# Graph stage of a graph/attention/expert layer: the edge part of the first layer computed for two node tiles at a time on 64-row halves, its bias added earlier

## The chip, the cores and the metric

The kernel runs on one core of one Trainium2 chip. The metric is the device time of one execution in microseconds (us). Three executions of the kernel before gave 1022.07, 1025.47 and 1028.08 us; the median, 1025.47 us, is the time before. All arithmetic named here is fp32 unless a row says bf16.

## The reference, cut to what matters

A layer over 3125 nodes with 256 features each, 53125 edges with 64 attributes each (`src` and `dst` node numbers), in four steps:

```python
xn = layernorm(x)                                   # 3125 x 256
# graph part
sums   = segment_sum(edge_attr, src, 3125)          # 3125 x 64
counts = segment_sum(ones, src, 3125)
agg    = sums / maximum(counts, 1)
h      = relu(concat([xn, agg, u[0] for every node])  W1 + b1)   # 448 -> 512
g      = h  W2 + b2                                # 512 -> 256
# linear-attention part over all nodes, 8 heads of 32
x      = x + g + attention(xn)
# expert part: router, softmax, best 2 of 8 experts, two-layer GELU network each
x      = x + moe(layernorm(x))
```

The rows of W1 fall into three blocks: 256 that multiply xn (the node part), 64 that multiply agg (the edge part) and 128 that multiply u[0] (the global part, the same for every node).

## The kernel before, in words

The 3125 nodes are 25 tiles of 125 (`T`, `P`). The whole program is written out by hand, one list of instructions for each engine, tied together by semaphores; there is no planner. The order is this.

- Edge sums, all the way to about 717 us. VectorE compares source numbers within groups of edges (`compare`, L1581), TensorE adds equal ones up (`dedup`, L1123), ScalarE copies the sums out (`sums_copy`, L750) and GpSimd scatter-adds each group of 128 edges to tables in HBM by an indirect DMA (L690, 368 of them).
- Beside it, first pass (25 tiles, to about 235 us): layernorm, keys and values, moments for the attention (VectorE's L1641 is its largest instruction). In tile 15 the global part is made: TensorE multiplies u0 by w1u, a row of 512 in PSUM (L1224), and VectorE adds it to the bias row, which lies as row 64 in `w1a` (L1698).
- Beside it, second pass (7 blocks of 3 or 4 tiles, in 56 rounds, to about 691 us): attention outputs. It also computes the node part of the graph layer: `hidden_x` (L1302) multiplies W1's node block with xn for a whole block of up to 500 nodes, a quarter (`m`) of the 512 outputs at a time, `h_copy` (L935) copies it from PSUM and a DMA stores it in HBM (`hpre_dram`, L938). The next `dedup` on TensorE waits for that copy, since it uses the same PSUM bank.
- When all scatters have landed, the tables are read back and averaged on VectorE (L1848 to L1859, `mean_ready`). TensorE turns the mean of each tile to 64 rows by 125 columns (L1434), ScalarE copies four tiles at a time to `aggT` (L1010), whose row 64 GpSimd set to one (L694).
- Graph stage (`gnn`, 25 tiles in a software pipeline of 29 iterations). In iteration t TensorE does `ha(t)` (L1445: 4 matmuls of 65 rows, w1a by aggT, 125 columns, into bank 1 or 2 in turn), `layer2(t-1)` (L1455, 4 matmuls of 128 rows, 256 columns), `tok_T(t-3)` (L1465) and `router(t-4)` (L1474). VectorE does `hsum(t)` (L1868: PSUM plus the stored node part, read back for two tiles at a time), `x2_of(t-1)` (L1875, then the statistics L1877 and L1879), `xl_of(t-2)` (L1887, L1888) and `lg_of(t-4)` (L1894). ScalarE does the ReLU (L1017), a square root (L1023) and two copies (L1030, L1037). `ha(t)` waits for `hsum(t-2)`, as each of its two banks holds one tile.
- Between iterations lies the routing of five batches of tiles (0-5, 6-11, 12-16, 17-21, 22-24): `lead`, `follow`, `weights` and `place` on VectorE in iterations t1+4 to t1+7 (L1911 to L1963), with t1 the end of the batch; an exponential on ScalarE (L1047), which needs another function table, and `ranks` on TensorE (L1489 to L1491).
- After `place` of a batch GpSimd sends its rows to the experts' regions, one indirect DMA for each tile and choice (L709, 50 in all). The expert stage (to the end) starts when the last has landed.

Of the kernel before, what the change touches and what calls it, by code (L numbers as in the profile page):

```python
# [9 lines left out]
ALU = mybir.AluOpType  # L10
# [4 lines left out]
def gps_layer(nc, x, src_col, src_row, edge_attr, u_in, W1, b1, W2, b2, WqkvT, bqkv, WprojT, bproj, temperature,  # L15
              routerT, ew1, eb1, ew2, eb2, out):
    N, C = x.shape
# [56 lines left out]
    with ctx:  # L74
        def sb(name, shape, dt=fp32):
            return ctx.enter_context(nc.sbuf_tensor(name, shape, dt))

        def sem(name):
            return ctx.enter_context(nc.semaphore(name))
# [23 lines left out]
        w1x = sb("w1x", [128, KC, HID])  # L103
        w1a = sb("w1a", [EA + 1, HID])
        w2s = sb("w2s", [128, MC, C])
# [114 lines left out]
        after_xl = r1_off[0]  # L220
        aggT = carve([EA + 1, T * P])
        cinv = carve([P, T])
# [94 lines left out]
        aggT_ready = sem("aggT_ready")  # L317
        agg_one = sem("agg_one")
        bias_ready = sem("bias_ready")
# [182 lines left out]
        def inside(t):  # L502
            return 0 <= t < T
# [6 lines left out]
        def _(sp):  # L510
# [45 lines left out]
            load_late(w1x[:, :, :], W1[0:C, :].rearrange("(k p) n -> p k n", p=128))  # L556
            load_late(w1a[0:EA, :], W1[C:C + EA, :])
            load_late(w1u[:, :], W1[C + EA:C + EA + 128, :])
            load_late(w1a[EA:EA + 1, :], b1.rearrange("(a n) -> a n", a=1))
            load_late(u0[:, :], u_in[0:1, :].rearrange("a p -> p a"), slow=True)  # L560
# [80 lines left out]
        def _(pool):  # L641
# [51 lines left out]
            pool.wait_ge(x1_ready, NP * NB)  # L693
            pool.memset(aggT[EA:EA + 1, :], 1.0).then_inc(agg_one, 1)  # L694
            for h in range(2):
# [31 lines left out]
        def _(act):  # L727
# [203 lines left out]
            def h_copy(b, m):  # L931
                n = width(b)
                act.wait_ge(h_ps, MC * b + m + 1)
                wait(act, hpre_stored[m % 2], 16 * (MC // 2 * b + m // 2))
                act.activation(hpre[:, m % 2, 0:n], bank(B0, 128, 0, n), ACT.Copy).then_inc(h_ready, 1)  # L935
                act.wait_ge(h_ready, MC * b + m + 1)
                c0 = BLK[b][0] * P
                act.dma_start(hpre_dram[:, m, c0:c0 + n], hpre[:, m % 2, 0:n]).then_inc(hpre_stored[m % 2], 16)  # L938
# [68 lines left out]
            for b in range(NBK):  # L1007
                nb = min(BPB, T - b * BPB) * P
                act.wait_ge(aggT_ps, b + 1)
                act.activation(aggT[0:EA, b * BPB * P:b * BPB * P + nb], bank((0, 7, 5, 6)[b % 4], EA, 0, nb),  # L1010
                               ACT.Copy).then_inc(aggT_ready, 1)
# [99 lines left out]
        def _(pe):  # L1111
# [104 lines left out]
            for t in range(T):  # L1216
# [5 lines left out]
                if t == 15:  # L1222
                    pe.wait_ge(w_loaded, 16 * 11)
                    mm(ps[EA:EA + 1, B1 * BANK:B1 * BANK + HID], lhsT=u0[:, :], rhs=w1u[:, :], start=True, stop=True).then_inc(brow_ps, 1)  # L1224
                if t == 16:
# [205 lines left out]
            for b in range(NBK):  # L1431
                wait(pe, aggT_ready, b - 3)
                for t in range(b * BPB, min((b + 1) * BPB, T)):
                    m = pe.transpose(bank((0, 7, 5, 6)[b % 4], EA, t % BPB * P, (t % BPB + 1) * P), table_sb(0)[:, t, 0:EA], ident[0:P, 0:P])  # L1434
                m.then_inc(aggT_ps, 1)
            pe.wait_ge(agg_one, 1)

            def ha(t, u):
                if not inside(t):
                    return  # L1440
                if t <= 1:
                    wait(pe, aggT_ready, NBK if t else 1)
                wait(pe, hsum_ready, t - 1)
                for m in range(MC):
                    z = mm(bank(1 + u, 128, m * P, (m + 1) * P), lhsT=w1a[:, m * 128:(m + 1) * 128], rhs=aggT[:, bass.ds(t * P, P)],  # L1445
                           start=True, stop=True)
                z.then_inc(ha_ps, 1)
# [29 lines left out]
            def gnn(t, u, k):  # L1477
                ha(t, u)
                layer2(t - 1, 1 - u)
                tok_T(t - 3, 1 - u)  # L1480
                router(t - 4, u)
# [74 lines left out]
        def _(v):  # L1556
# [126 lines left out]
            for t in range(T):  # L1683
# [10 lines left out]
                if t == 15:  # L1694
                    v.wait_ge(w_loaded, 16 * 11)
                    link(v.tensor_scalar(temp[:, :], temp[:, :], SC2, None, ALU.mult))
                    v.wait_ge(brow_ps, 1)
                    v.tensor_tensor(w1a[EA:EA + 1, :], ps[EA:EA + 1, B1 * BANK:B1 * BANK + HID], w1a[EA:EA + 1, :], ALU.add).then_inc(brow_read, 1)  # L1698
                if t in (17, 20):
# [162 lines left out]
            def hsum(t, u, k):  # L1862
                if not inside(t):
                    return
                wait(v, ha_ps, t + 1)
                wait(v, hpre_back[k % 2], k // 2 * 16 + 16)
                wait(v, gnn_ps, t - 1)
                v.tensor_tensor(hs[:, u, :].rearrange("p (m n) -> p m n", m=MC), bank(1 + u, 128, 0, MC * P).rearrange("p (m n) -> p m n", m=MC),  # L1868
                                hpre2[:, k % 2, :, u * P:(u + 1) * P], ALU.add).then_inc(hsum_ready, 1)

# [224 lines left out]
```

## Time and profile before

| | us |
|---|---|
| median of three executions | 1025.47 |
| the profiled execution: its time | 1024.87 |
| its span, first to last instruction | 1023.1 |
| busy in the span: TensorE (PE) / VectorE (DVE) / ScalarE (ACT) / GpSimd (POOL) | 844.8 / 627.1 / 416.3 / 710.3 |
| graph stage, by L1445's first and L1455's last start | 740.7 to 830.4 |
| mean granted TensorE clock | 0.904 |

Times in the rows below are microseconds from the start of the span unless marked ns. The granted clock is a share of full speed and has two levels, 1.00 (2.4 GHz) and 0.50 (1.2 GHz); a number between them is a mean over a stretch. The profile records an fp32 matmul as two instructions, each streaming its columns once; this text calls each a pass. PEld is TensorE's loading of weights. The time outside the span, 1.8 us, is start and end of the program.

### The profile page before, as it was taken

What the parts mean: (1) busy time and instruction counts of PE and PEld (TensorE: products, weight loads), DVE (VectorE), ACT (ScalarE), POOL (GpSimd) and SP (SyncE); (2) the same over time, 40 slices, a digit from 0 to 9 for tenths busy, and PEclk for the clock granted to TensorE, in tenths of its full rate; (3) what the DMA queues carried; (4) which work ended last, traced back from release to release, by engine and by line L of the source; (5) the groups of instructions that cost most, each with busy time, mean ns of one, the idle gap of its engine ahead of it and who ended that gap; (6) DMA issues with size and microseconds to landing.
All of it is one profiled execution on the core that took longest, in us unless ns stands there. A gap on an engine that the chain in (4) does not pass through costs nothing.

```text
span 1023.1 us, 19212 instructions
## 1 busy us (share of the span) xinstructions
PE 844.8 (83%) x6172; PEld 520.5 (51%) x6172; DVE 627.1 (61%) x2123; ACT 416.3 (41%) x1087; POOL 710.3 (69%) x511
## 2 busy tenths in 40 slices
PE   3888888979999999999999999990299961999930
PEld 2434333435445545544455555550288851899930
DVE  3899997994665464454645646650567773655534
ACT  3554553332554334343343434330145440666620
POOL 4688888888888888887788888888312568544430
PEclk7799998996999999999999999995599975999975
DMA  9865663555655554555555555334952424344449
GB/s 288 196 108 81 94 117 41 81 88 76 129 74 81 111 92 67 69 86 100 100 88 80 106 83 110 42 28 42 274 170 82 145 88 135 107 132 125 130 131 276
DMA packets 146342, 113.86 MB, mean 111 GB/s; under 512 B 109023, under 2 KB 132131, under 8 KB 146118
## 3 DMA queue, kind: packets, MB, share of 16 engines
q1 hardware_dynamic: 81156, 72.53, 25.3%
q0 software_dynamic: 58080, 25.70, 24.2%
q10 hardware_dynamic: 7010, 14.42, 4.4%
q8 instruction: 52, 0.85, 0.4%
q14 instruction: 44, 0.36, 0.1%
HBM read 72.52 MB, written 41.17 MB: 111 GB/s over the span
## 4 chain that ended last, share of the span: by engine, by line
PE 42%; DVE 20%; POOL 19%; issue 9%; DMA 6%; ACT 3%; ACTq 0%; SPq 0%; POOLq 0%; DVEq 0%
POOL edge_sums L690 17%; DVE r2t L1641 9%; PE ps L1315 5%; PE ps L1526 5%; PE ps L1537 5%; PE ps L1123 4%; DVE same L1581 3%; PE ps L1455 3%; PE ps L1251 3%; PE ps L1302 3%; DMA r2t<-expert_outputs 2%; PE ps L1265 2%; POOL routed_rows L709 2%; PE ps L1191 1%; DMA edges<-in_edge_attr 1%
## 5 line engine op out<-in xcount | busy, mean ns | idle before, releaser
L690 POOL DMA_INDIRECT edge_sums<-sums,addr x368 | 576.3, 1566 | 135.2 <-issue 108.8
L1678 DVE TENSOR_SCALAR oh<-node,dsrc 128x500 bf16<-128x500 int16 (+1 forms) x336 | 100.6, 360 | 49.8 <-PE ps L1315 49.1
L916 ACT ACTIVATE r<-ps 128x500 f32<-128x500 f32 (+1 forms) x224 | 103.4, 548 | 66.8 <-PE ps L1251 66.7
L1315 PE MATMUL ps<-oh,r2t 128*64 128x500 bf16 (+1 forms) x1008 | 114.6, 360 | 1.5 <-DVE oh L1678 1.4
L1123 PE MATMUL ps<-edges,same 128*128 128x65 f32 x736 | 103.5, 287 | 10.4 <-ACT sums L750 6.2
L1123 PEld LDWEIGHTS ps<-edges,same 128*128 128x128 f32 x736 | 93.9, 200 | 34.8 <-issue 19.1
L1641 DVE TENSOR_TENSOR r2t<-ps,r 125x4096 f32<-125x4096 f32 x25 | 110.3, 4413 | 0.0
L1581 DVE SCALAR_TENSOR_TENSOR same<-srow,src_f,below 128x128 f32<-128x128 int32 x368 | 105.7, 344 | 6.7 <-DMA srow<-in_src_row 5.3
L721 POOL DMA_INDIRECT expert_outputs<-r x56 | 54.5, 974 | 55.9 <-DVE r L2034 49.5
L1170 PE MATMUL ps<-r2t,r 125*32 125x512 f32 x400 | 60.7, 732 | 31.4 <-DVE r2t L1641 31.4
L1315 PEld LDWEIGHTS ps<-oh,r2t 128*64 128x64 bf16 x1008 | 49.6, 110 | 64.8 <-issue 38.7
L750 ACT ACTIVATE sums<-ps 128x260 f32<-128x260 f32 x92 | 36.5, 398 | 109.0 <-PE ps L1123 105.6
L709 POOL DMA_INDIRECT routed_rows<-r,row_idx x25 | 24.7, 988 | 59.3 <-ACT edges L1037 41.0
L1526 PE MATMUL ps<-r 128*128 128x128 f32 x448 | 60.8, 279 | 1.5 <-ACT r L1072 1.5
L1251 PE MATMUL ps<-r,pick 32*128 32x500 f32 (+1 forms) x448 | 61.1, 591 | 0.0
L1537 PE MATMUL ps<-r2t,r 128*128 x224 | 57.6, 380 | 0.0
L1526 PEld LDWEIGHTS ps<-r 128*128 128x128 f32 x448 | 56.1, 196 | 2.0 <-ACT r L1063 1.1
L1265 PE MATMUL ps<-r,mq 128*32 128x500 f32 (+1 forms) x448 | 53.6, 550 | 0.0
L2024 DVE COPY r<-r2t 128x512 f32 x56 | 33.4, 596 | 32.7 <-issue 17.7
L1161 PE MATMUL ps<-wqkv,r 128*125 128x512 f32 x100 | 53.2, 656 | 0.0
L1455 PE MATMUL ps<-w2s,r 128*125 128x256 f32 x200 | 48.9, 388 | 4.0 <-ACT r L1017 4.0
L1072 ACT ACTIVATE r<-ps,step_bias 128x128 f32<-128x128 f32 x112 | 35.2, 366 | 38.6 <-PE ps L1537 38.6
(284 smaller groups left out, 1377.2 us busy)
## 6 DMA issues: line engine op xcount, KB each, us to landing
srow<-in_src_row SPq DMA_DIRECT2D x46, 512.0 KB, 6.1
edges<-in_edge_attr SPq DMA_DIRECT2D x23, 512.0 KB
r<-routed_rows SPq DMA_DIRECT2D x56, 129.0 KB, 2.1
r<-hpre_rows SPq DMA_DIRECT2D x12, 500.0 KB, 4.2
edge_sums<-sums,addr POOLq DMA_INDIRECT x368, 3.2
r2t<-in_ew SPq DMA_DIRECT2D x4, 1024.0 KB, 10.0
hpre_rows<-r ACTq DMA_DIRECT2D x16, 250.0 KB, 2.3
edge_sums<-r SPq DMA_DIRECT2D x4, 884.0 KB, 14.3
```

What stands on the lines that cost most here:

```text
L690: pool.indirect_dma_start(out=tables[k], out_offset=bass.IndirectOffsetOnAxis(ap=addr[:, j:j + 1], axis=0), in_=sums[:, j % OR, :], in_off ...
L916: act.activation(phT[:, R % 2, h, 0:n], bank(BP[h], 128, 0, n), ACT.Square).then_inc(pair_squares, 1)
L1123: m = mm(bank(b, 128, k * F, (k + 1) * F), lhsT=same[:, j % SR, :], rhs=edges[:, h, j % CH, :], start=True, stop=True)
L1251: m = mm(bank(BP[h], 128, 0, n), lhsT=pick2[D * h:D * (h + 1), c * 128:(c + 1) * 128], rhs=qnT[D * h:D * (h + 1), b % 2, g, 0:n], start=Tr ...
L1265: m = mm(ps[D * h:D * (h + 1), BY * BANK:BY * BANK + n], lhsT=mq[:, g, c, D * h:D * (h + 1)], rhs=phT[:, R % 2, h, 0:n], start=False, stop ...
L1315: m = mm(ps[EA * a:EA * (a + 1), BD * BANK:BD * BANK + n], lhsT=parts3[:, (DCH - 1 - 2 * w // DW) * DW + (2 * w + a) % DW, s, :], rhs=oh[: ...
L1455: z = mm(bank(3 + u, P, 0, C), lhsT=hs[:, u, m * P:(m + 1) * P], rhs=w2s[:, m, :], start=(m == 0), stop=(m == MC - 1))
L1526: z = mm(bank(2 + h % 2, 128, m * 128, (m + 1) * 128), lhsT=w1_now[:, h % 2, k, m * 128:(m + 1) * 128], rhs=xsT[:, h % 2, k * 128:(k + 1) ...
L1537: z = mm(bank(6 + h % 2, 128, 0, C), lhsT=hT[:, h % 2, k * 128:(k + 1) * 128], rhs=ew2_s[:, k, bass.ds(col, C)], start=(k == 0), stop=(k = ...
L1581: v.scalar_tensor_tensor(same[:, j % SR, :], srow[:, c % 2, j % RH * 128:(j % RH + 1) * 128], src_f[:, j:j + 1], below[:, :], ALU.is_equal ...
L1641: v.tensor_tensor(phi[:, u], heads(bank(BK[u], P, 0, C), None).unsqueeze(2).to_broadcast([P, H, OFF, D]), turned(kdup[:, u, :, :], 1, H, 2 ...
L1678: v.tensor_scalar(oh[:, (2 * i + a) % OHS, 0:nt * P].rearrange("p (t n) -> p t n", t=nt), node16[:, 0:nt, :], dsrc[:, 2 * w + a:2 * w + a ...
```

## The change

1. `aggT` holds each tile's mean twice, on rows 0 to 63 and 64 to 127, and so does `w1a` with W1's edge block (a second load). The row of ones is gone. To get the two copies in PSUM, the transpose L1434 becomes two ordinary products with the identity, one on array columns 0 to 63, one on 64 to 127. ScalarE's L1010 copies 128 rows instead of 64.
2. `ha(k)` computes a pair of tiles in every other iteration: again 4 matmuls, now of 64 rows and 250 columns, quarters 0 and 2 on the array's rows 0 to 63 into bank 1, quarters 1 and 3 on rows 64 to 127 into bank 2. It waits until `hsum` has read both tiles of the pair before. `hsum(t)` reads its half of both banks.
3. Bias and global part go out of w1a: `hid_b` is a 128 x 4 tile. b1 is loaded into it (elements of 4 bytes), the global part is made by 4 matmuls of one column each, VectorE adds 128 x 4 instead of 1 x 512, and `h_copy` adds the column of `hid_b` (Identity with a bias operand instead of Copy).

```diff
-        w1a = sb("w1a", [EA + 1, HID])
+        w1a = sb("w1a", [2 * EA, HID])
+        hid_b = sb("hid_b", [128, MC])
-        aggT = carve([EA + 1, T * P])
+        aggT = carve([2 * EA, T * P])
 # SyncE, loads of the first pass
-            load_late(w1a[0:EA, :], W1[C:C + EA, :])
+            for a in range(2):
+                load_late(w1a[a * EA:(a + 1) * EA, :], W1[C:C + EA, :])
-            load_late(w1a[EA:EA + 1, :], b1.rearrange("(a n) -> a n", a=1))
+            load_late(hid_b[:, :], b1.rearrange("(m p) -> p m", p=128), slow=True)
 # GpSimd
-            pool.memset(aggT[EA:EA + 1, :], 1.0).then_inc(agg_one, 1)
 # ScalarE
+                if b == 0 and m == 0:
+                    act.wait_ge(brow_read, 1)
-                act.activation(hpre[:, m % 2, 0:n], bank(B0, 128, 0, n), ACT.Copy).then_inc(h_ready, 1)
+                act.activation(hpre[:, m % 2, 0:n], bank(B0, 128, 0, n), ACT.Identity, bias=hid_b[:, m:m + 1]).then_inc(h_ready, 1)
-                act.activation(aggT[0:EA, b * BPB * P:b * BPB * P + nb], bank((0, 7, 5, 6)[b % 4], EA, 0, nb),
+                act.activation(aggT[:, b * BPB * P:b * BPB * P + nb], bank((0, 7, 5, 6)[b % 4], 128, 0, nb),
 # TensorE, tile 15 of the first pass
-                    pe.wait_ge(w_loaded, 16 * 11)
-                    mm(ps[EA:EA + 1, B1 * BANK:B1 * BANK + HID], lhsT=u0[:, :], rhs=w1u[:, :], start=True, stop=True).then_inc(brow_ps, 1)
+                    pe.wait_ge(w_loaded, 16 * 12)
+                    for m in range(MC):
+                        z = mm(bank(B1, 128, m, m + 1), lhsT=w1u[:, m * 128:(m + 1) * 128], rhs=u0[:, :], start=True, stop=True)
+                    z.then_inc(brow_ps, 1)
 # TensorE, the turned means
-                    m = pe.transpose(bank((0, 7, 5, 6)[b % 4], EA, t % BPB * P, (t % BPB + 1) * P), table_sb(0)[:, t, 0:EA], ident[0:P, 0:P])
+                    for a in range(2):
+                        c0 = (0, 7, 5, 6)[b % 4] * BANK + t % BPB * P
+                        m = mm(ps[a * EA:(a + 1) * EA, c0:c0 + P], lhsT=table_sb(0)[:, t, 0:EA], rhs=ident[0:P, 0:P], start=True, stop=True)
-            pe.wait_ge(agg_one, 1)
-            def ha(t, u):
+            def ha(k):
+                t0, t1 = 2 * k, min(2 * k + 2, T)
+                w = (t1 - t0) * P
-                if t <= 1:
-                    wait(pe, aggT_ready, NBK if t else 1)
-                wait(pe, hsum_ready, t - 1)
+                if k <= 1:
+                    wait(pe, aggT_ready, NBK if k else 1)
+                wait(pe, hsum_ready, t0)
                 for m in range(MC):
-                    z = mm(bank(1 + u, 128, m * P, (m + 1) * P), lhsT=w1a[:, m * 128:(m + 1) * 128], rhs=aggT[:, bass.ds(t * P, P)],
-                           start=True, stop=True)
+                    a, j = m % 2, m // 2
+                    z = mm(bank(1 + a, 128, j * w, (j + 1) * w), lhsT=w1a[a * EA:(a + 1) * EA, m * 128:(m + 1) * 128],
+                           rhs=aggT[a * EA:(a + 1) * EA, t0 * P:t1 * P], start=True, stop=True)
             def gnn(t, u, k):
-                ha(t, u)
+                if u == 0 and inside(t):
+                    ha(k)
 # VectorE, tile 15 of the first pass
-                    v.wait_ge(w_loaded, 16 * 11)
+                    v.wait_ge(w_loaded, 16 * 12)
-                    v.tensor_tensor(w1a[EA:EA + 1, :], ps[EA:EA + 1, B1 * BANK:B1 * BANK + HID], w1a[EA:EA + 1, :], ALU.add).then_inc(brow_read, 1)
+                    v.tensor_tensor(hid_b[:, :], bank(B1, 128, 0, MC), hid_b[:, :], ALU.add).then_inc(brow_read, 1)
 # VectorE, hsum
-                wait(v, ha_ps, t + 1)
+                wait(v, ha_ps, k + 1)
-                v.tensor_tensor(hs[:, u, :].rearrange("p (m n) -> p m n", m=MC), bank(1 + u, 128, 0, MC * P).rearrange("p (m n) -> p m n", m=MC),
-                                hpre2[:, k % 2, :, u * P:(u + 1) * P], ALU.add).then_inc(hsum_ready, 1)
+                w = (min(2 * k + 2, T) - 2 * k) * P
+                own = ps[:, BANK:3 * BANK].rearrange("p (a z) -> p a z", a=2)[:, :, 0:2 * w].rearrange("p a (j n) -> p j a n", j=2)
+                v.tensor_tensor(hs[:, u, :].rearrange("p (j a n) -> p j a n", j=2, a=2), own[:, :, :, u * P:(u + 1) * P],
+                                hpre2[:, k % 2, :, u * P:(u + 1) * P].rearrange("p (j a) n -> p j a n", j=2), ALU.add).then_inc(hsum_ready, 1)
```

## Rows read from the trace of the kernel before

**Rows 1.** Chain of waits, in order of time: start us, us, what.

```profile
492.05 1.58 POOL edge_sums L690
...
715.01 8.07 DMA edge_sums<-sums,addr
...
735.48 5.42 PE ps L1434 x25
```

**Rows 2.** Waits by releaser from 742 to 832: us in total, times, longest us.

```profile
DVE x_res L1875 <- PE ps L1455: 13.7, 14, 1.9
...
PE ps L1455 <- ACT r L1017: 4.0, 5, 1.0
```

**Rows 3.** GpSimd in order of time: start us, us, what, in brackets its idle time.

```profile
807.81 0.97 POOL L709 DMA_INDIRECT routed_rows<-r,row_idx  x1 [6.83 <-DVE row_idx L1961]
...
827.95 0.97 POOL L709 DMA_INDIRECT routed_rows<-r,row_idx  x1 [5.06 <-DVE row_idx L1961]
...
860.49 0.97 POOL L709 DMA_INDIRECT routed_rows<-edges,row_idx  x1 [0.30 <-issue]
```

**Rows 4.** Stretches: us, busy us of PE, PEld, DVE, ACT, POOL, clock, DMA share, GB/s.

```profile
735.50:741.40 5.90, 5.90 (x29) 5.14 (x30) 5.24 (x8) 3.59 (x7) 5.83 (x2) 0.51 1.10 353
741.40:770.50 29.10, 28.51 (x189) 25.96 (x189) 18.41 (x55) 12.06 (x31) 3.66 (x3) 1.00 0.49 154
...
806.20:809.70 3.50, 3.50 (x13) 2.88 (x13) 2.60 (x11) 2.02 (x5) 1.58 (x2) 0.51 0.14 13
...
867.00:900.00 33.00, 31.32 (x212) 28.92 (x213) 18.71 (x55) 19.89 (x60) 19.38 (x15) 0.94 0.37 110
```

**Rows 5.** PE in order of time from 640 us: start us, us, what, passes.

```profile
641.77 0.91 PE L1251 MATMUL ps<-r,pick 32*128 32x375 f32 x8
642.62 0.90 PE L1262 MATMUL ps<-r,wlow 128*128 128x375 f32 x2
643.36 0.79 PE L1263 MATMUL ps<-r,wlow 128*128 128x375 f32 x2
644.08 0.84 PE L1265 MATMUL ps<-r,mq 128*32 128x375 f32 x8
644.85 0.54 PE L1282 MATMUL ps<-ident,r 125*128 125x125 f32 x3
```

**Rows 6.** Chain of waits within the graph stage.

```profile
757.10 0.34 PE ps L1474 x4
757.44 0.99 PE ps L1445 x8
758.43 1.73 PE ps L1455 x8
760.37 0.34 PE ps L1474 x4
...
792.09 0.43 DVE x_res L1875
```

**Rows 7.** DVE in order of time around the start of the stage.

```profile
742.15 0.68 DVE L1868 TENSOR_TENSOR r<-ps,r 128x500 f32<-128x500 f32 x1 [0.90 <-DVE row_idx L1972]
...
770.02 0.42 DVE L1875 TENSOR_TENSOR x_res<-ps,x_res 125x256 f32<-125x256 f32 x1 [1.01 <-PE ps L1455]
```

**Rows 8.** ScalarE's groups by shape: busy us, mean ns, idle us before.

```profile
L1017 ACT ACTIVATE r<-r 128x500 f32<-128x500 f32 x25 | 15.5, 622 | 22.9 <-DVE r L1868 22.9
...
L767 ACT ACTIVATE r<-x_res,neg_mean 125x256 f32<-125x256 f32 x25 | 12.3, 496 | 0.0
...
L757 ACT ACTIVATE r<-x_res 125x256 f32<-125x256 f32 x25 | 10.0, 403 | 0.0
```

**Rows 9.** PE around 805 us, in order of time.

```profile
805.48 3.12 PE L1455 MATMUL ps<-w2s,r 128*125 128x256 f32 x8 [1.00 <-ACT r L1017]
```

**Rows 10.** Waits by releaser from 246 to 490: us in total, times, longest us.

```profile
PEld ps L1123 <- ACT r L935: 6.0, 15, 0.4
```

**Rows 11.** DVE in order of time around 161 us.

```profile
160.64 0.69 DVE L1698 TENSOR_TENSOR w1a<-ps,w1a 1x512 f32<-1x512 f32 x1 [3.42 <-PE ps L1224]
```

More of the change, by code:

```diff
@@ L317, in gps_layer @@
         aggT_ready = sem("aggT_ready")
-        agg_one = sem("agg_one")
         bias_ready = sem("bias_ready")
@@ L1433, in _ @@
                 for t in range(b * BPB, min((b + 1) * BPB, T)):
-                    m = pe.transpose(bank((0, 7, 5, 6)[b % 4], EA, t % BPB * P, (t % BPB + 1) * P), table_sb(0)[:, t, 0:EA], ident[0:P, 0:P])
+                    for a in range(2):
+                        c0 = (0, 7, 5, 6)[b % 4] * BANK + t % BPB * P
+                        m = mm(ps[a * EA:(a + 1) * EA, c0:c0 + P], lhsT=table_sb(0)[:, t, 0:EA], rhs=ident[0:P, 0:P], start=True, stop=True)
                 m.then_inc(aggT_ps, 1)
-            pe.wait_ge(agg_one, 1)
-            def ha(t, u):
-                if not inside(t):
-                    return
-                if t <= 1:
-                    wait(pe, aggT_ready, NBK if t else 1)
-                wait(pe, hsum_ready, t - 1)
+            def ha(k):
[4 more added lines that the diff above has]
+                wait(pe, hsum_ready, t0)
                 for m in range(MC):
-                    z = mm(bank(1 + u, 128, m * P, (m + 1) * P), lhsT=w1a[:, m * 128:(m + 1) * 128], rhs=aggT[:, bass.ds(t * P, P)],
-                           start=True, stop=True)
+                    a, j = m % 2, m // 2
+                    z = mm(bank(1 + a, 128, j * w, (j + 1) * w), lhsT=w1a[a * EA:(a + 1) * EA, m * 128:(m + 1) * 128],
+                           rhs=aggT[a * EA:(a + 1) * EA, t0 * P:t1 * P], start=True, stop=True)
                 z.then_inc(ha_ps, 1)
```

## The prediction

> **What bounds the kernel now.** I read the chain of waits first. From 492 us on it is GpSimd alone, scatter after scatter, up to the last edge sum at 715.01; then the tables come back, are averaged, and the means are turned on TensorE from 735.48 for 5.42 us [rows 1]. So what changes on another engine between 492 and 715 costs nothing, but what delays TensorE or VectorE before 492 moves the scatters and all that follows.
>
> Then the waits of the graph stage (742 to 832). VectorE stood idle for TensorE 14 times, 13.7 us in all; TensorE waited for the ReLU only 4.0 us [rows 2]. The stage looks like TensorE's, but 14 waits in 25 tiles say that only somewhat more than half of them go at its pace; near the routing of a batch VectorE is the pace, and a faster TensorE gives nothing there.
>
> Last, who waits for the stage. GpSimd starts the second batch's rows at 807.81, the third's at 827.95, and from there it runs without a gap to its last at 860.49 [rows 3]: 26 scatters, 1.28 us apart. So the expert stage comes earlier by just as much as `place` of the third batch (iteration 24) does. The second batch's 12 scatters end 15.4 us after 807.81, at 823.2, so up to 4.7 us of such a gain can be taken.
>
> **The change, part by part.**
>
> *Turning the means.* Before: 25 single passes, 5.42/25 = 0.217 us each, at the half clock (mean 0.51 from 735.5 to 741.4, 1.00 after) [rows 1, 4]. After: 50 products of two passes, the two of a tile on different column groups. That such groups run beside one another L1265 shows: four fp32 products on four groups, 8 passes of 375 columns, take 0.77 us to the next start [rows 5]; a pass of 256 columns costs 1.73/8 = 0.216 us [rows 6], so 375 cost 0.316, and 8 in a row would take 2.5. So a tile costs 2 x 0.217 = 0.43 us at half clock, half of it at full. The clock rose 5.9 us after this work began; in that time 13.6 tiles are done, the other 11.4 take 2.5: 8.4 us. Bounds: at the start of the expert stage (867.2) the clock was low for 0.06 x 2 x 33 = 4.0 us [rows 4]; that gives 7.4; no rise at all 10.8; no overlap of the groups 13.8.
> Then the first pair's `ha` takes 1.0 us. So `hsum(0)` can start 9.4 us after 735.48; before, VectorE started it at 742.15, after a memset [rows 7], 6.7 us after. I take **+2.7 us** (bounds +1.7 and +5.1, +8.1 without overlap), nearest to the clock's own row. ScalarE's copies go over 128 rows with as many columns as before and have more time between them: 0.
>
> *A pair's edge part.* Before, 0.99 us a tile up to the start of L1455 [rows 6]: 1.98 for two. After: quarters 0 and 1 beside one another, then 2 and 3: 4 passes of 250 columns in a row, 4 x 0.21 = 0.84 us. That row groups overlap L1251 shows (four groups of 32 rows, 8 passes, 0.85 us to the next start) [rows 5]. There the price of leaving the full array is seen too: 0.85 for two passes' columns, 0.63; and L1262 with L1263, full array between two split ones, 1.46 for 1.26. Each stay in a layout costs 0.2 us beyond its columns. A pair brings one stay on halves and one more on the full array: 1.24 us, and 0.1 where L1455 now follows the router directly. Two iterations lasted 2 x 3.27 = 6.54 us [rows 6]; now 6.54 - 1.98 + 1.34 = 5.90: **0.6 us less per pair**. Bounds: 1.1 (stays free) and -0.2 (halves don't overlap: 8 x 0.21 + 0.5 = 2.2).
> The Trainium skill, "TensorEngine Tiling (Array Packing)", Key Properties, says that a change of the tiling mode, unlike a change of the tile, drains the engine. The trace agrees with its 0.2 us a stay. By the "up to 2x" of that page's Theoretical Speedup alone a pair would save 0.99 us, and the stage's term below would be -5 instead of -3.1.
>
> *Where that counts.* VectorE was idle 1.01 us in an iteration of 3.27 [rows 7]: its own work is 2.26. `layer2(t)` can follow `layer2(t-2)` after VectorE's 2.26, the ReLU's 0.62 [rows 8], L1455's 1.73 and some 0.2 between engines: 4.8 us. Two iterations now last 5.9: TensorE stays the pace there. The new wait (`ha(k)` for both `hsum` of the pair before) holds up `layer2`, `tok_T` and `router`. In the steady run `hsum(2k-1)` ends 2.3 us after `layer2(2k-3)`, and TensorE reaches `ha(k)` 0.55 + 1.73 + 0.55 = 2.8 us after it: no wait. In iteration 4, with no router yet, it waits some 0.5.
> First run, `layer2(0)` to `x2_of(8)` at 770.02 [rows 7]: four pairs, -0.6 each, but for the one with that wait, -0.1: -1.9 us. Batch 0's routing, tiles 9 to 12, at VectorE's pace: 0. Tiles 13 and 14, up to 792.09 [rows 6]: one iteration without `ha`, -0.6. Batch 1's routing, 0. Tiles 18 and 19 likewise -0.6, then VectorE's pace up to `place` of the third batch. Sum **-3.1 us**, where 12 pairs would give 7.
> `hsum` reads 500 elements as before, now over two banks: 0. No row has such a pattern; the same engine adds as many elements over one bank in 0.68 [rows 7], and I allow 0.05 either way, 1 us in all.
>
> *The clock.* It fell once in the stage, from 806.2 for 3.4 us [rows 4], while L1455, which had waited 1.00 us for the ReLU, took 3.12 [rows 9]. 3.4 us at half clock do the work of 1.7. The change takes about 1 us of work off TensorE in every pair, so in VectorE's stretches it idles more. I keep one fall; none is -1.7, each further one +1.7.
>
> *`h_copy` with a bias operand.* L767 (Square with one) takes 0.496 us, L757 (Copy, same shape) 0.403 [rows 8]: +0.1. Between 246 and 490 TensorE's next `dedup` waited for this copy 15 times [rows 10]: 15 x 0.1 = **+1.5 us**. Bounds 0 (a copy from PSUM need not behave like these) and 3.0 (twice the rows' difference). After 492 GpSimd's backlog hides it; without that, 28 x 0.1 = 2.8.
>
> *Global part.* Four products of one column are 8 passes, as short as the router's, 0.34/4 = 0.09 each [rows 6]: 0.7 us, against two passes of 512 columns, 0.86. VectorE waits 3.42 us for it in either case, then adds 128 x 4 instead of 0.69 us for one row [rows 11], some 0.2; VectorE is on the chain there: **-0.5 us** (bounds -0.7 and 0). That wait was for TensorE and not for the loads, so the second w1a load and b1's small elements, two issues more or longer on SP's queue ahead of the edge blocks, cost 0 while that stays; a row block late by 2 us would be +2. GpSimd's memset (L694) goes from a time in which it waited for the means: 0.
>
> **Sum.** 2.7 - 3.1 + 1.5 - 0.5 = +0.6 us. The profiled execution took 1024.87 (span 1023.1, 1.8 around it): 1025.5. It lies 0.6 below the median of three, so I forecast **1026 us**. A change under 0.5% (5.1 us) is about what a measurement of this kernel cannot tell from none.
>
> **The rivals.**
> - *TensorE's gain counts in every tile.* For: in the stage it waits only 4.0 us. Against: VectorE's stretches. 12 x 0.6 = 7.2 for 3.1: 1022; with the early rise (-1.0) and no fall (-1.7), 1019. Chance 0.13.
> - *An early rise and no fall, rest as forecast:* 1026 - 2.7 = 1023. Chance 0.15.
> - *The clock takes it back; slower.* Place: the stretches before the exponentials, where TensorE waits for the ReLU. Two further falls give 1029.4, three and no rise while the means are turned (+2.4) 1033.5; it is slower than now from the first fall on and measurable from the third. For: the fall at 806. Against: five such waits, up to 1.0 us [rows 2], and one fall. Chance 0.14.
> - *Halves do not overlap:* +3.1 and 12 x 0.2: 1031.5. Against: L1251 [rows 5]. Chance 0.06.
> - The forecast itself 0.52, its own range 1023.5 to 1028.5.
>
> Range 1020 to 1032. Faster by over 0.5%: 0.09, most of the first rival; slower: 0.15, from the third and fourth and their mixtures; within 0.5%: 0.76.
>
> **What would show it.** L1434: 100 passes in some 8 us, the two column groups starting together. L1445: 100 passes of 250 columns, both halves starting together, and L1455's groups 5.9 us apart by pairs in the first run. VectorE's idle time for L1455 down from 13.7 to about 10 us. From the last edge scatter to the last row scatter 145.5 us as now, within 1. L767's 0.1 on L935, and the last edge scatter at 716. It is wrong if the way between those two scatters changes by over 4 us, or if the last edge scatter moves by over 3.

## The result, and the profile after

| | before | after | ratio of the runs, 95% interval |
|---|---|---|---|
| first comparison, median of 11 runs each | 1024.96 (1021.0 to 1028.08) | 1029.25 (1023.6 to 1032.72) | 1.0053 [1.0034, 1.0071] |
| second comparison, 35 and 12 runs | 1022.72 | 1027.81 | 1.0041 [1.0015, 1.0066] |
| profiled execution (span) | 1024.87 (1023.1) | 1029.76 (1027.7) | |

The change costs 4.3 us in the first comparison and 5.1 in the second, by the medians; by the ratios it is 5.4 and 4.2. One of the 35 runs of the second comparison took 2090.72 us; it is left out of the ratio. The forecast was 1026 us, +0.5; the time lies inside the range of 1020 to 1032. The bound of 0.5% that was called no difference lies inside both intervals: neither comparison tells on which side of it the change is. So the forecast held as a number, but most of the loss was not in its sum.

The two profiled executions differ by 4.9 us. They can be laid along GpSimd's landmarks [rows 1, 3]. GpSimd after, in order of time (last edge scatter, first row scatter of batches 1 to 3, last row scatter):

```profile
717.00 1.55 POOL L691 DMA_INDIRECT edge_sums<-sums,addr  x1 [0.30 <-issue]
...
788.67 1.03 POOL L709 DMA_INDIRECT routed_rows<-r,row_idx  x1 [41.73 <-ACT edges L1039]
...
810.03 0.97 POOL L709 DMA_INDIRECT routed_rows<-r,row_idx  x1 [6.13 <-DVE row_idx L1970]
...
830.50 0.97 POOL L709 DMA_INDIRECT routed_rows<-r,row_idx  x1 [5.44 <-DVE row_idx L1970]
...
862.97 0.97 POOL L709 DMA_INDIRECT routed_rows<-edges,row_idx  x1 [0.30 <-issue]
```

Up to the last edge scatter +2.0 (715.01 before), from there to the last row scatter +0.5 (145.5 before, 146.0 now), and from there to the end of the span +2.1 (162.6, now 164.7); the other 0.3 lies outside the span. The last is not the change's: a second profile of the kernel before has 164.3 there, the kernels of the experiments 162.8 to 165.6.

The start of the graph stage after (start us, us, what; the rows that answer [rows 7]):

```profile
737.37 8.49 PE L1440 MATMUL ps<-ident,srow 125*64 125x125 f32 x100 [43.50 <-DVE srow L1866]
...
745.79 1.11 PE L1451 MATMUL ps<-r,w1a 64*128 64x250 f32 x8
...
747.00 1.27 DVE L1877 TENSOR_TENSOR r<-ps,r 128x500 f32<-128x500 f32 x2 [3.86 <-issue]
...
748.39 1.99 PE L1461 MATMUL ps<-w2s,r 128*125 128x256 f32 x8 [1.49 <-ACT r L1019]
```

L1440 is the turning, L1451 the edge part, L1877 `hsum`, L1461 `layer2`. From the first turning to the first `hsum` it is 9.6 us, before 6.7. The steady stretch, TensorE after:

```profile
755.64 1.11 PE L1451 MATMUL ps<-r,w1a 64*128 64x250 f32 x8 [0.16 <-DVE r L1877]
756.69 1.99 PE L1461 MATMUL ps<-w2s,r 128*125 128x256 f32 x8
758.52 0.38 PE L1471 MATMUL ps<-ident,r 125*128 125x125 f32 x2
758.73 0.50 PE L1480 MATMUL ps<-wr,r 128*125 128x8 f32 x4
759.09 1.97 PE L1461 MATMUL ps<-w2s,r 128*125 128x256 f32 x8
...
761.54 1.11 PE L1451 MATMUL ps<-r,w1a 64*128 64x250 f32 x8
```

A pair takes 761.54 - 755.64 = 5.90 us, as worked out. Waits after, 745 to 834 (us in total, times, longest), beside [rows 2]:

```profile
DVE x_res L1884 <- PE ps L1461: 10.9, 9, 2.2
...
PE ps L1461 <- ACT r L1019: 5.8, 6, 1.7
```

VectorE waits less for TensorE (13.7 before), TensorE waits more for the ReLU (4.0). And the clock, TensorE alone in stretches (us, PE busy, clock, DMA share, GB/s):

```profile
780.00:790.00 10.00, 8.11 (x51) 1.00 0.18 51
...
800.00:810.00 10.00, 7.88 (x45) 0.91 0.34 104
810.00:820.00 10.00, 9.29 (x55) 0.92 0.45 142
820.00:830.00 10.00, 7.96 (x48) 0.94 0.29 91
830.00:834.00 4.00, 4.00 (x18) 0.73 0.19 67
```

The clock is at 1.2 GHz from 808.3 for 3.4 us and again from 828.8 for 3.4; before it fell once [rows 4]. Both falls follow stretches in which TensorE stood idle a fifth of the time (7.88 and 7.96 busy of 10). That is what went before them and not yet their cause: "pairs on the full array" below is as idle and does not fall.

### The profile page after: what moved, and what is told of

Read it like the earlier page. It is cut to its first block, busy times and chain, and to the rows that moved or that the text cites. A ratio compares the mean times of both kernels' runs of the same rounds, so it can differ in the third digit from the quotient of the medians.

```text
span 1027.7 us, 19184 instructions
## 1 busy us (share of the span) xinstructions
PE 844.0 (82%) x6157; PEld 513.6 (50%) x6157; DVE 625.5 (61%) x2123; ACT 418.4 (41%) x1087; POOL 708.6 (69%) x510
## 4 chain that ended last, share of the span: by engine, by line
PE 41%; DVE 22%; POOL 17%; issue 7%; DMA 7%; ACT 2%; SPq 2%; ACTq 0%; POOLq 0%; DVEq 0%
POOL edge_sums L691 16%; DVE r2t L1648 10%; PE ps L1319 5%; PE ps L1533 5%; PE ps L1544 5%; PE ps L1125 4%; DVE same L1588 3%; PE ps L1461 3%; PE ps L1255 3%; DMA r2t<-expert_outputs 3%; PE ps L1306 3%; DMA edge_sums<-sums,addr 3%; PE ps L1269 2%; SPq L533 2%; PE ps L1193 1%
## 5 line engine op out<-in xcount | busy, mean ns | idle before, releaser
L1172 PE MATMUL ps<-r2t,r 125*32 125x512 f32 x400 | 58.5, 709 | 31.4 <-DVE r2t L1648 31.4
L709 POOL DMA_INDIRECT routed_rows<-r,row_idx x25 | 24.7, 988 | 60.0 <-ACT edges L1039 41.7
L1461 PE MATMUL ps<-w2s,r 128*125 128x256 f32 x200 | 51.9, 406 | 5.8 <-ACT r L1019 5.8
```

The costliest lines, as they stand in the source:

```text
L1461: z = mm(bank(3 + u, P, 0, C), lhsT=hs[:, u, m * P:(m + 1) * P], rhs=w2s[:, m, :], start=(m == 0), stop=(m == MC - 1))
```

## The experiments

Three questions: is the turning mis-sized, is the bias operand, or does the clock take back what the pairs give? In the expectations "A" is the operand, "B" the graph stage with its turning and clock. Where one of them names another run by its label, e2 is "tiles on halves", e6 "fast turning", e7 "kept busy" and e9 "bias in the ReLU". Each kernel was timed in five rounds beside before, in three groups: plain copy, bias only, turning only and tiles on halves (median of before 1024.29), then full array, fast turning, kept busy and late blocks (1023.23), then the ReLU, combined and the two repeats (1022.72). Only the ratios can be compared between groups. The first comparison of after is its own group (1024.96). The intervals reach 1.6 to 2.6 us to either side, so two ratios that differ by under some 0.0027 (2.8 us) are not clearly apart. The landmarks come from one profile of each. The last two columns are the time from the first `hsum` to the third batch's first row scatter, and for how long falls of the clock that began in it lasted (for fast turning the rest of the low stretch before the stage).

| kernel | median | ratio, 95% interval | last edge scatter | hsum to batch 3 | low |
|---|---|---|---|---|---|
| before | | | 715.0 | 85.8 | 3.4 |
| before, again | 1023.89 | 1.0003 [0.9980, 1.0027] | 712.6 | 84.4 | 0 |
| bias only | 1026.63 | 1.0022 [1.0004, 1.0041] | 717.6 | 84.5 | 0 |
| turning only | 1025.09 | 1.0017 [1.0001, 1.0033] | 712.0 | 84.5 | 0 |
| fast turning | 1021.19 | 0.9982 [0.9963, 1.0002] | 712.3 | 85.9 | 4.3 |
| after | 1029.25 | 1.0053 [1.0034, 1.0071] | 717.0 | 83.5 | 6.8 |
| after, again | 1027.81 | 1.0041 [1.0015, 1.0066] | 717.3 | 86.8 | 13.6 |
| plain copy | 1025.46 | 1.0025 [1.0006, 1.0043] | 710.5 | 83.5 | 6.8 |
| bias in late blocks | 1026.57 | 1.0031 [1.0009, 1.0052] | 714.1 | 86.6 | 13.6 |
| bias in the ReLU | 1025.31 | 1.0003 [0.9979, 1.0027] | 712.3 | 86.8 | 13.6 |
| tiles on halves | 1028.20 | 1.0041 [1.0022, 1.0061] | 717.4 | 87.0 | 17.0 |
| kept busy | 1024.06 | 1.0008 [0.9987, 1.0029] | 716.9 | 82.0 | 0 |
| pairs on the full array | 1031.05 | 1.0064 [1.0044, 1.0084] | 716.8 | 86.3 | 0 |
| combined | 1019.31 | 0.9960 [0.9937, 0.9982] | 709.7 | 84.5 | 0 |

**Plain copy.** After, with

```diff
-    act.activation(hpre[...], bank(B0, 128, 0, n), ACT.Identity, bias=hid_b[:, m:m + 1])
+    act.activation(hpre[...], bank(B0, 128, 0, n), ACT.Copy)
```

> The kernel after, but h_copy is a plain Copy again, so bias and global part are left out of the result. What is open: the ledger gave +0.6 us, the timing says some 4.3 to 5.5. Theory A (the bias operand is the larger part: 0.09 us on each copy, handed on by TensorE's waits before 490 us): this kernel is 1.5 us or more faster than the kernel after, its last edge scatter comes 1.5 us earlier than there (717.0), L937 takes 0.59 instead of 0.68 us. Theory B (the graph stage is where the time went, by the slow turning of the means and more falls of the clock): no more than 1 us faster than the kernel after, and still 3 to 4 us slower than the kernel before.

1025.46, ratio 1.0025 against 1.0053 for after: the operand is worth 2.9 us by this, twice the term forecast, with the two intervals some 2.7 us to either side. Bias and global part are missing from this kernel's result.

**Bias only.** Before, with `hid_b` (its load, the four products, VectorE's addition and the operand on `h_copy`), row 64 of `w1a` zero; turning and edge part as before.

> The kernel before with the third part of the change alone: hid_b, Identity with a bias operand in h_copy, four products of one column, 128 x 4 addition; row 64 of w1a is set to zero, so the ones row adds nothing. Edge part, turning and hsum as before. Theory A: 1 us (prediction: +1.5 - 0.5) up to 3 us slower than the kernel before. Theory B: within 1 us of it.

+2.3 us by the ratio (0.4 to 4.2), with the gain of the global part in it. Its last edge scatter is late by as much as after's.

**Turning only.** Before, with L1434's transpose made two products as in after:

> The kernel before with the turning of the means alone changed: 50 products with the identity instead of 25 transposes, the second half of the rows not used. The start of the stage is then late by what the 100 passes cost: layer2(0) 2.5 to 3.2 us later after mean_ready than before. Prediction: 2.7 us slower than the kernel before, since nothing takes it back. Theory B: 3 us or more, with the clock as in the kernel before. If below 1.5 us, the start of the stage has slack that I have not seen.

+1.7 us by the ratio, from 0.1 to 3.4. The first `hsum` stands 8.3 us after the turning's start (before 6.7, again 5.9), since the clock rose early in this profile, 3.3 us after the turning began.

**Tiles on halves.** After, with tile 2k on rows 0 to 63 and tile 2k+1 on rows 64 to 127. The means are written densely, so that 13 transposes of 128 columns turn them:

```diff
-    mm(ps[a * EA:(a + 1) * EA, c0:c0 + P], lhsT=table_sb(0)[:, t, 0:EA], rhs=ident[0:P, 0:P])
+    pe.transpose(bank(...), means[:, 2 * k * EA:2 * k * EA + w], ident[0:P, 0:P])
...
+    mm(bank(1 + a, 128, m * P, (m + 1) * P), lhsT=w1a[a * EA:(a + 1) * EA, ...],
+       rhs=aggT[a * EA:(a + 1) * EA, k * P:(k + 1) * P])
```

> The kernel after with another use of the halves: tile 2k of a pair on rows 0 to 63, tile 2k+1 on rows 64 to 127, so the means are not needed twice. VectorE writes them without gaps, and 13 transposes of 128 columns, one pass each, turn two tiles at a time (13 x 0.217 = 2.8 us at half clock, against 25 x 0.217 = 5.4 before and 8.5 after). A pair's edge part is 16 passes of 125 columns, 8 in a row on each half, 0.9 us. Both theories: start of the stage 5 to 6 us earlier than in the kernel after, except that VectorE is held up until 742 by the memset, which leaves some 4.8 us. Theory A: 4.8 faster than after, so equal to the kernel before or 1 us faster. Theory B: the same, if the clock rises no later; if the clock rises later since it sees only short transposes, 1 to 3 us less.

The turning takes 2.97 us instead of 8.49, yet the total is after's. The rows show why (this kernel, in order of time):

```profile
738.70 2.97 PE L1441 MATMUL ps<-ident,oh 125*128 125x125 f32 x13 [44.45 <-DVE oh L1866]
...
738.79 5.47 POOL L699 MEMSET r<- 32x6450 f32 x1 [19.84 <-DVE oh L1866]
...
739.61 4.68 DVE L1978 TENSOR_SCALAR r<-reg_start,ident 125x8 f32<-125x8 f32 x1
741.60 2.08 PE L1451 MATMUL ps<-r,w1a 64*128 64x125 f32 x16
...
744.50 1.27 DVE L1875 TENSOR_TENSOR r<-ps,r 128x500 f32<-128x500 f32 x2
```

A VectorE operation on 125 x 8 elements lasts 4.68 us, up to the end of GpSimd's memset beside it, and `hsum`, whose products are done by 743.7, comes behind it. It lasts 4.68 us beside that memset in the kernels before and after as well; after, the longer turning hides it. TensorE idles, and at 747 the clock falls.

**Fast turning.** Before, with those 13 transposes, both halves copied to rows 0 to 63, and VectorE's set-up (L1978 above and its neighbours) moved ahead of the tables' addition:

> The kernel before, with another way of turning the means: VectorE writes them densely, two tiles of 64 channels side by side, so that 13 transposes of 128 columns turn them instead of 25 of 64; ScalarE takes the two halves out of PSUM into the same 64 rows; the edge part waits for its batch alone; VectorE's small set-up operations come ahead of the addition of the tables. No halves, no bias operand. If the time from mean_ready to the first hsum is a term of its own in the total, as in the kernel after where it cost +3.2 us, then here TensorE's turning takes about 3 us instead of 5.4 and the total is 2 to 3 us below before: ratio 0.997 to 0.998. If instead the stage has slack of its own there (VectorE's stretches absorb a start that is earlier), or if the shorter turning leaves the clock low for longer, the ratio is 0.999 to 1.001. A ratio above 1.001 speaks against both.

1.8 us faster by the ratio, but its interval still holds no difference. The first `hsum` stands 4.7 us after the turning's start, before 6.7 and (again) 5.9. The profile shows little of a gain beyond that: the clock rose only 9.1 us after the turning began (before 5.9, again 4.2), so the stage's first tiles went at 1.2 GHz, and from the start of the turning to the third batch's rows it is 90.6 us, in "before, again" 90.3. Moved ahead, the 125 x 8 operation has no memset beside it and takes 0.26 us. TensorE at the start (us, busy, clock), and that operation:

```profile
733.00:742.00 9.00, 8.89 (x36) 0.50 1.10 350
```

```profile
687.04 0.26 DVE L1866 TENSOR_SCALAR r<-reg_start,ident 125x8 f32<-125x8 f32 x1
```

**Pairs on the full array.** After, with rows 64 to 127 of `w1a` zero, so that the same four products contract over all 128 rows, one after another:

```diff
-    mm(bank(...), lhsT=w1a[a * EA:(a + 1) * EA, m * 128:(m + 1) * 128], rhs=aggT[a * EA:(a + 1) * EA, t0 * P:t1 * P])
+    mm(bank(...), lhsT=w1a[:, m * 128:(m + 1) * 128], rhs=aggT[:, t0 * P:t1 * P])
```

> The kernel after, but the edge part of a pair runs on the full array: rows 64 to 127 of w1a are zero, the aggregates stay doubled, and each product contracts over all 128 rows. The result is the same. The four quarters no longer run beside one another. Theory C (halves let the clock fall): the two profiles of kernels with halves had 2 falls of the clock in the graph stage (3 with tiles on halves), the three without had 0 or 1; then this kernel has 0 or 1, and what it loses in the pairs (4 x 0.21 us more columns, less the two stays of 0.2: +0.4 to +0.8 us a pair, some 2 to 4 us where TensorE sets the pace) is given back by 3 to 6 us of clock: batch 3's first row scatter 110 to 113 us after the last edge scatter (after: 113.5), the ratio to before below that of after by up to 0.002. Theory D (falls come by chance of the timing, not by the layout): 1 to 2 falls as in after, and batch 3's rows 115 to 117 us after the last edge scatter; the ratio 1.007 to 1.009.

**Kept busy.** After, with

```diff
+    if any(t1 + 5 <= t <= t1 + 7 for t0, t1 in BATCHES[:3]):
+        for _ in range(1 + u):
+            mm(bank(7, 128, 0, C), lhsT=ones[:, :], rhs=w2s[:, 0, :], start=True, stop=True)
     layer2(t - 1, 1 - u)
```

> The kernel after, with one or two extra products of 256 columns (0.9 us a tile on average 1.3; into a bank that nobody reads) ahead of layer2 in three tiles of each of the first three batches, where TensorE otherwise waits for the ReLU while VectorE routes a batch. Their results are not used. Theory C2 (the further falls of the clock are what keeps the pair's gain from arriving): fewer falls in the graph stage than the 2 of after, from the last edge scatter to batch 3's first rows 110 to 112 us instead of 113.5, and the ratio to before 0.002 to 0.003 below that of after. Theory B2 (falls cost little, the loss is the slow turning and the bias operand alone): the extra products are hidden where TensorE waits, or cost up to 2 us; 113 to 115.5 us, ratio as after or up to 0.002 above.

These two bear on the clock. TensorE in the same stretches, first the full array, then the halves kept busy:

```profile
780.00:790.00 10.00, 7.96 (x45) 1.00 0.19 51
...
800.00:810.00 10.00, 8.55 (x52) 1.00 0.48 157
810.00:820.00 10.00, 9.16 (x50) 1.00 0.37 116
820.00:830.00 10.00, 7.90 (x47) 1.00 0.38 118
```

```profile
780.00:790.00 10.00, 9.69 (x58) 1.00 0.20 52
...
800.00:810.00 10.00, 9.69 (x58) 1.00 0.33 104
810.00:820.00 10.00, 9.29 (x57) 1.00 0.56 169
820.00:830.00 10.00, 8.78 (x58) 1.00 0.18 65
```

Neither falls. On the full array the pairs cost 4.3 us more than on halves (86.3 against 82.0), so the halves do overlap and pay; 1.9 of the 4.3 go on computing in pairs at all (84.4 with single tiles). With the added products the time from `hsum` to batch 3 is 82.0 us, and the total 3.4 (against the second comparison) to 4.6 us (the first) below after by the ratios, each give or take some 3, though TensorE does more. The added work sits in TensorE's waits: 9.69 us busy from 780 to 790, in after 8.11. But the full array is as idle as after (7.96, 8.55 and 7.90 of 10, in after 8.11, 7.88 and 7.96) and kept its clock in its one profile. So idle time alone does not tell when the clock falls. Whether the layout on halves or the moments at which TensorE waits decide it, no run shows.

The price of a fall can be read off GpSimd's first scatter of batches 2 and 3, here of "kept busy" and of "plain copy" (low at 779 to 783 and 820 to 824):

```profile
809.89 0.97 POOL L709 DMA_INDIRECT routed_rows<-r,row_idx  x1 [6.12 <-DVE row_idx L1973]
828.83 0.97 POOL L709 DMA_INDIRECT routed_rows<-r,row_idx  x1 [3.89 <-DVE row_idx L1973]
```

```profile
803.97 0.97 POOL L709 DMA_INDIRECT routed_rows<-r,row_idx  x1 [7.79 <-DVE row_idx L1970]
822.91 0.97 POOL L709 DMA_INDIRECT routed_rows<-r,row_idx  x1 [3.89 <-DVE row_idx L1970]
```

| us | `hsum` to batch 1 | batch 1 to 2 | batch 2 to 3 | low from |
|---|---|---|---|---|
| before | 43.6 | 22.05 | 20.14 | 806.2 |
| before, again | 43.6 | 22.04 | 18.80 | none |
| kept busy | 41.7 | 21.35 | 18.94 | none |
| after | 41.7 | 21.36 | 20.47 | 808.3, 828.8 |
| plain copy | 41.7 | 22.94 | 18.94 | 779, 820 |
| after, again | 41.7 | 24.62 | 20.52 | 788 (twice as long), 812, 832.5 |

The pairs gain 1.9, 0.7 and -0.1 us in the three parts. A low stretch of 3.4 us costs 1.5 to 1.6, one of 6.8 costs 3.3, and the last one before batch 3's rows costs nothing.

**After and before, again.**

> The kernel after, unchanged, for a second profiled execution and a second interval beside the same runs of before. The edge part ended between 710.5 and 717.6 us in the profiles so far, and kernels with the same code up to there differed by 3 us. If the bias operand is the whole of its +2.0 us, the last edge scatter stands 2 to 3 us later than in another profile of before; if the profiles differ by where the clock happened to fall, it may stand anywhere from 714 to 718. From there to the third batch's first rows: 113.5 us with two falls, 112 without. Ratio 1.003 to 1.006.

> The kernel before, unchanged, for a second profiled execution, and as a zero for the intervals: ratio 0.998 to 1.002. Last edge scatter between 712 and 715 us (715.0 in the first profile, 712.0 and 712.3 in two kernels that differ from it only after that scatter); from there to the third batch's first rows 112.9 us with one fall in the stage, 111.5 without.

After again had four low stretches' worth, 13.6 us, and 86.8 instead of 83.5 (the last of them, from 832.5, is not shown):

```profile
788.00:795.00 7.00, 7.00 (x25) 0.51 0.46 138
812.00:815.50 3.50, 3.50 (x13) 0.51 0.05 2
```

Before again had none and ended its edge part at 712.6, earlier than 715.0. The ratio of after came again, but from the edge part to batch 3 it took 117.2 us, where 113.5 were expected with two falls: there were more. Its last edge scatter at 717.3 is 4.7 us later than this one of before, where 2 to 3 were expected of the operand; the two differ in more than the operand (see the last section). From the last edge scatter to the last row scatter this pair takes 143.3 and 149.6 us.

**Bias in late blocks.** After, with the plain Copy for blocks 0 to 3 (no bias, no global part there) and the operand from block 4 on:

> The kernel after, but h_copy is the plain Copy for the first four blocks (bias and global part are left out there) and has its bias operand from block 4 on. Theory A1 (the bias operand costs where TensorE's dedup waits for the copy before 492 us, the first four blocks; later GpSimd's backlog hides it): as with the plain copy everywhere, 2 to 3 us below after, ratio to before 1.002 to 1.003, last edge scatter 2 to 3 us earlier than after for the same state of the clock. Theory A2 (each of the 28 copies costs wherever it stands, or the cost is the wait of the first copy for hid_b's sum): ratio 1.004 to 1.0055.

Ratio 1.0031, between the two theories and with an interval that holds both; last edge scatter 3 us earlier, which is the A1 side. GpSimd's two waits in this kernel stand ahead of its first copy with an operand (533.79), so they are not the operand's:

```profile
481.19 1.55 POOL L691 DMA_INDIRECT edge_sums<-sums,addr  x1 [1.99 <-ACT sums L750]
...
490.65 1.57 POOL L691 DMA_INDIRECT edge_sums<-sums,addr  x1 [2.34 <-issue]
```

**Bias in the ReLU.** After, with the plain Copy everywhere and

```diff
-    act.activation(hs[:, u, :], hs[:, u, :], ACT.Relu).then_inc(hs_ready, 1)
+    for m in range(MC):
+        act.activation(hs[:, u, m * P:(m + 1) * P], hs[:, u, m * P:(m + 1) * P], ACT.Relu, bias=hid_b[:, m:m + 1]).then_inc(hs_ready, 1)
```

> The kernel after, but b1 and the global part are added by the ReLU of the graph stage instead of the copy of the node part: h_copy is a plain Copy, and the ReLU of a tile is four operations of 125 columns, each with its column of hid_b; layer2's four products each wait for their own quarter. The result is the same. Theory A (the operand on h_copy costs 2 to 3 us, because TensorE waits for that copy; in the graph stage TensorE is the pace and the ReLU has room): ratio to before 1.002 to 1.003, as with the plain copy and no bias, and x2_of advances 5.9 us a pair in the first run as in after. Rival (four ReLUs of some 0.25 us and their starts are later than one of 0.62, and VectorE's stretches pass it on: +0.3 us a tile in the 12 tiles at VectorE's pace): from layer2(0) to batch 3's rows +3 us, ratio 1.004 to 1.006.

1.0003 against 1.0041 for after beside it: 3.9 us less, the two intervals some 3.6 to either side. Four ReLUs last 1.27 us, but `layer2` starts on the first quarter; `hsum` to batch 3 is 86.8 at 13.6 us of low clock, as in "bias in late blocks" (86.6) with one ReLU. So the 3 us that the rival names are there, but they are the falls', and the bias is nearly free.

**Combined.** Dense means on halves, set-up moved ahead, bias in the ReLU, added products:

> All that the runs point to in one kernel: edge part by tile pairs with tile 2k on rows 0 to 63 and tile 2k+1 on rows 64 to 127 (as in e2), means turned by 13 transposes of 128 columns, each batch waited for alone, VectorE's set-up ahead of the tables' addition (as in e6), the bias in the ReLU by quarters (as in e9), and one or two extra products in three tiles of the first three batches that keep TensorE busy (as in e7; their results are not used). From the single runs: turning -1.5 to -2 us against before, pairs -2.5, no fall of the clock -1.3 where before had one, global part -0.5, extra products 0: 4 to 6 us faster, ratio 0.994 to 0.996 if the terms add up and the ReLU by quarters is free; 0.997 to 0.999 if it is not (VectorE's stretches pass +0.3 us a tile on). hs0 to batch 3's first rows 82 us in the first case (before 85.8, before without a fall 84.5), 85 in the second.

1019.31, ratio 0.9960 [0.9937, 0.9982]: faster than before by 3.4 us and than after by 8.5, by the medians. Its rows:

```profile
729.86 2.97 PE L1442 MATMUL ps<-ident,oh 125*128 125x125 f32 x13 [45.63 <-DVE oh L1877]
...
734.44 1.27 DVE L1886 TENSOR_TENSOR r<-ps,r 128x500 f32<-128x500 f32 x2 [4.64 <-PE ps L1452]
...
818.98 0.97 POOL L710 DMA_INDIRECT routed_rows<-r,row_idx  x1 [4.62 <-DVE row_idx L1979]
```

Turning to `hsum` 4.6 us, as hoped. From `hsum` to batch 3 it took 84.5 and not 82: the terms did not all add up, and which of the parts kept the pairs' 2.5 us is open. No run tried the parts two by two.

## Why the prediction was right or wrong, step by step

- **Turning the means, +2.7: right.** 100 passes took 8.49 us (8.4 worked out) and the column groups ran beside one another. First turning to first `hsum` came out at 9.6, 3.0 more than before; the second pair of profiles gives 9.3 against 5.9, 3.4 more, since both kernels vary with the moment at which the clock rises. Over all eight profiles with this turning it is 8.2 to 9.7, on average 8.9, over the three with the old one (before, before again, bias only) 6.1: 2.8 more. The single change showed +1.7 in the total (0.1 to 3.4).
- **A pair's edge part, -0.6: right.** 5.90 us a pair. Both halves started together (6 ns apart), with passes of 0.21.
- **Where that counts, -3.1: right in kind, 0.6 too large.** `layer2(0)` to `x2_of(8)` went from 26.5 to 24.5 us (-2.0 for -1.9), tiles 13 and 14 gave -0.65 (-0.6), and tiles 18 and 19 nothing (-0.6 forecast). Without falls on either side it is 82.0 against 84.4, **-2.5**. The new wait of `ha` for the pair before took 2.5 us in three places, where the sum had 0.5 in one. With half of 1.98 us saved in every pair the prediction's own count gives -5.4, where it names -5.
- **The clock, one fall in both: this step failed.** It was put as "I keep one fall", with 1.7 us for each further one. The fall in the profile before was itself the exception: four other profiles with the old edge part and the one with pairs on the full array have none; of the six with halves and no added products every one has 6.8 to 17.0 us. The price was nearly right, 1.5 to 1.6 us for each 3.4; but the last stretch before batch 3's rows costs nothing, since the routing of that batch did not come later for it. So the falls cost 1.5 us in the first profile of after (one counts), 1.6 in "plain copy" and 4.6 to 4.9 in the three with 13.6 us low: from more than half of the pairs' 2.5 to nearly twice that. Set beside its own fall, the first profile of before hides this: 1.3 us there and 1.5 here. The rival "the clock takes it back" was given 0.14 and named the place, the stretches before the exponentials where TensorE waits for the ReLU. By its own signs the prediction was wrong in the second pair of profiles, where the way between the two scatters grew by 6.3 us (over 4) and the last edge scatter moved by 4.7 (over 3), and right in the first (+0.5 and +2.0).
- **`h_copy`'s operand, +1.5 (0 to 3.0): too small, by about half.** The instruction got slower by just the 0.1 us: ScalarE's groups after and with the plain copy,

```profile
L937 ACT ACTIVATE r<-ps,hid_b 128x500 f32<-128x500 f32 x16 | 10.8, 677 | 39.6 <-PE ps L1306 39.6
```

```profile
L937 ACT ACTIVATE r<-ps 128x500 f32<-128x500 f32 x16 | 9.4, 588 | 39.2 <-PE ps L1306 39.2
```

0.089 us. The Trainium skill, "ScalarE: Activation LUTs", What ACT_TABLE_LOAD costs, gives about 93 ns for each pointer operand of this kind; the trace agrees, from PSUM as well. TensorE's waits for it between 246 and 490 rose by only 0.8:

```profile
PEld ps L1125 <- ACT r L937: 6.8, 14, 0.5
```

What came on top is not shown as a cause, but one thing goes with it, a fall of the clock at 460. All six profiles with the operand in the early blocks have it, none of the eight others. After and "bias in the ReLU", 460.0 to 463.8:

```profile
460.00:463.80 3.80, 3.80 (x22) 0.55 0.95 214
```

```profile
460.00:463.80 3.80, 3.80 (x21) 1.00 1.08 245
```

Behind it GpSimd stood idle for 2.1 and 2.4 us:

```profile
483.90 1.55 POOL L691 DMA_INDIRECT edge_sums<-sums,addr  x1 [2.08 <-ACT sums L750]
...
493.44 1.55 POOL L691 DMA_INDIRECT edge_sums<-sums,addr  x1 [2.42 <-issue]
```

These waits are not the operand's. The first profile of before has them too (1.75 and 2.33 us), and so has "bias in late blocks" (1.99 and 2.34). One or both, or in "bias only" a third, stand in all nine profiles in which the clock was low from 228 to 245 us, and in none of the five others; and that stretch is over before the first `h_copy` starts (264.51 in after). So landmarks are best compared within the nine: there the last edge scatter stands at 716.8 to 717.6 with the operand in the early blocks and at 712.3 to 715.0 without, 3.4 us on average. In the five others, all without the operand, it stands at 709.7 to 712.6. In total time the operand is worth 2.9 us ("plain copy") to 3.9 ("bias in the ReLU"), where 1.5 was forecast; the intervals would allow 1.5 as well. Why the fall at 460 comes with the operand is open.

- **Global part, -0.5:** VectorE's addition took 0.16 us for 0.69 and stands 1.0 us earlier (159.69). "Bias only" at +2.3 against an operand of 2.9 to 3.9 leaves -0.6 to -1.6 for it, a difference well inside the intervals.
- **The sum.** Operand with global part +2.3 and turning +1.7 by their single runs, pairs -2.5 by the profiles without falls, falls +1.5 to +4.8, less up to 1.3 where before has its own: 1.7 to 6.3, for 4.3 and 5.1 measured. The terms come partly from ratios with intervals of 1.6 to 1.9 us to either side; that the measured loss lies near the middle is in part luck. And that the forecast stayed in its range is luck too: its sum lacked 1.4 to 2.4 us of the operand, 0.6 of the pairs and up to 4.8 of falls, and the range was wide enough for them.

## What to carry to other kernels

Where an engine runs close to its partner's pace, a layout that takes work off it can come with falls of its clock: look at the clock before counting the gain, and try cheap products in the waits. A fall cost nearly half its length where the next stage waited for this engine (1.5 to 1.6 us of 3.4), and nothing where it did not. A small cost on a copy that another engine waits for can count for more than its nanoseconds (0.09 us each here, 2.9 to 3.9 in all). And compare at least two profiles of the kernel before: one fall of the clock was in the single profile, and the forecast took it for the rule.

## What was not expected of the hardware

- The clock in a stage with short waits. The Trainium skill, "TensorE: Matmul & The Clock Gate", A second HAM failure mode, tells of a kernel whose short idles between groups of products let the clock go up and down. The traces here agree that the clock goes up and down in such a stage (after has low stretches at 808.3 and 828.8) and show its price, 1.5 to 1.6 us for 3.4 us at 1.2 GHz. They also hold a case against idle time as the only cause: with products added (9.69 us busy from 780 to 790 for 8.11) the clock stayed up, but on the full array it stayed up at 7.96 as well.
- One program has more than one course through its first pass. In "before, again" the mean clock from 228 to 246 was 0.91, in before 0.54; the first `h_copy` starts at 258.7 and 266.0 and the last edge scatter at 712.6 and 715.0. Of the 14 profiles nine take the slow course, all six with the operand in the early blocks among them, though it parts before the first such copy. Whether the change makes that course more frequent is open:

```profile
228.00:246.00 18.00, 14.45 (x92) 0.54 0.51 78
```

```profile
228.00:246.00 18.00, 16.15 (x135) 0.91 0.57 86
```

- A small VectorE operation (125 x 8) beside a GpSimd memset of 5.47 us lasted 4.68 us, in "fast turning", without the memset beside it, 0.26; memsets of VectorE's own beside the same one took 0.1.
